# Attention scores: the order of the four matmuls in a group

## The chip, the cores and the metric

The kernel runs on one core of a Trainium2 chip. The metric is the device time of one execution, in microseconds (us); of several executions the median is given.

## The reference, cut to what matters

A gated cross-attention layer with a mixture of experts behind it, on 8 batches of 512 tokens with 256 features, in float32:

```
q, k, v = heads of layernorm(x) @ Wq + bq, ctx @ Wk + bk, ctx @ Wv + bv   # 16 heads of 16 features
attn = softmax(clip(q @ k.T / 4, -10000, 10000))
x = x + tanh(g_xattn) * ((attn @ v) @ Wo + bo)
x = x + tanh(g_ffn) * experts(layernorm(x))      # 8 experts, gated with a threshold over all tokens
```

The change lies in the scores, `q @ k.T`. The experts, which take most of the time, are the same in both kernels.

## The kernel before, in words

The program has stages with a barrier between them: a projection (`build_project`), attention (`build_attend`), two stages that only run when a flag asks for them, and the experts (`build_experts`). In the profile attention lies between about 105 and 577 us.

Attention goes through 8 batches (`b`), in each through 4 groups of 4 heads (`g`), and in each group through 4 steps (`k`, one for each block of 128 keys). Each step needs two kinds of score for the 4 heads of a group:

- A transposed score, T0 to T3 (`scores_T`, line 825): 128 keys by 512 queries into a bank of `ps_t`. ScalarE takes its exponential into `probs_T` (line 1072), and this frees the bank. There are three banks, so a T waits for the exponential of the third T before it (semaphore `exp_done`).
- A plain score, S0 to S3 (`scores`, line 815), for the group that comes two groups later: 128 queries by 512 keys into a bank of `ps_s`. VectorE reduces it to its row minimum (line 958), which later serves to keep the exponentials in range, and this frees the bank. Here too are three banks, so an S waits for the reduction of the third S before it (`low_done`).

Both have a contraction of 48 or 49 rows and take only half of the array's rows: even heads lie on rows 0 to 63 and odd heads on rows 64 to 127 (`half_rows`). Two matmuls on different halves can run at the same time. The plain scores take the heads in the order 1, 0, 3, 2 (`SCORE_HEADS`), so S0 lies on the upper half, and S1 on the lower one.

TensorE's order is written out by hand (lines 906 to 930). A step is: a first four of matmuls (T0, S0, T1, S1), the product of the previous step's probabilities with the values (`probs_v`, line 836, eight matmuls), a shared unit if there is one, a second four (T2, S2, T3, S3), and again a shared unit if there is one. TensorE works through this list in its order; a matmul that waits holds those behind it.

A shared unit is a small piece of work that isn't scores and that uses one common bank, `ps_m`: transposing the minima (`low`, line 842), the output heads (`out`, 847), the attention rows (`rows`, 853), the output projection (`y`, 861), transposes of the residual stream (`x2T`, 868, and `xnT`, 874), and the gate's logits (882, 889). The table `SHARED` says after which half step each one stands. Each waits until the unit before it has been taken out of the bank by ScalarE or VectorE. VectorE's own queue is in order too: in each step two reductions, then what it takes of a shared unit (`normalise`, line 981; `add_residual`, 991; `layer_norm`, 1008; `split`, 1016), then two more reductions. ScalarE has two exponentials, its unit, and two exponentials.

Of the kernel before, what the change touches and what calls it, by code (L numbers as in the profile page):

```python
# [55 lines left out]
def wait(eng, sem, value):  # L56

    if isinstance(value, int) and value <= 0:
        return
    eng.wait_ge(sem, value)  # L60
# [505 lines left out]
def exists(b):  # L566

    return not isinstance(b, int) or 0 <= b < BATCH
# [20 lines left out]
def half_rows(j, rows):  # L589

    return slice(j % 2 * 64, j % 2 * 64 + rows)


def group_after(b, g, steps):

    return b + (g + steps) // GROUPS, (g + steps) % GROUPS


def bank_of(turn, at):

    return (turn + at) % BANKS


def turn_after(turn, g, steps):

    return turn + (g + steps) // GROUPS
# [9 lines left out]
def build_attend(nc, io, scratch, keep):  # L616
    with ExitStack() as ctx:
# [61 lines left out]
        def group_no(b, g):  # L679
            return b * GROUPS + g  # L680

        def free_after(b, at):

            return b * PRODUCTS + at - BANKS + 1
# [121 lines left out]
        def _(pe):  # L806
            def scores(b, g, t, i, turn):

                at = (g * TT + t) * GROUP + i
                j = SCORE_HEADS[i]  # L810
                rows = half_rows(j, ROWS)
                if t == 0 and i == 0:
                    pe.wait_ge(qk_loaded[g], b * QK_PIECES * 16 + QK_PIECES * 16)
                wait(pe, low_done, free_after(b, at))
                pe.matmul(ps_s[bank_of(turn, at)][:], q_st[g][rows, j // 2, t * P:(t + 1) * P], k_st[g][rows, j // 2, :],  # L815
                          start=True, stop=True).then_inc(scores_in_psum, 1)

            def scores_T(b, g, k, j, turn):

                at = (g * TT + k) * GROUP + j  # L820
                if k == 0 and j == 0:
                    pe.wait_ge(rows_sent, group_no(b, g) * 32 + 32)
                wait(pe, exp_done, free_after(b, at))
                rows = half_rows(j, ROWS + 1)
                pe.matmul(ps_t[bank_of(turn, at)][:], k_st[g][rows, j // 2, k * P:(k + 1) * P], q_st[g][rows, j // 2, :],  # L825
                          start=True, stop=True).then_inc(t_in_psum, 1)

            def probs_v(b, g, k):

                n = quad_no(b, g, k)  # L830
                if k == 0:
                    pe.wait_ge(v_loaded[g], b * 16 + 16)
                    wait(pe, o_copied, group_no(b, g))
                pe.wait_ge(exp_done, n * GROUP + GROUP)
                for j in range(GROUP):
                    mm = pe.matmul(ps_o[32 * j:32 * j + VW, :], v_st[g][:, k, j, :], probs_T[k][:, j, :],  # L836
                                   start=(k == 0), stop=(k == TT - 1))
                mm.then_inc(pv_done, 1)
# [57 lines left out]
            def shared(b, unit):  # L896
                if not unit or not exists(b + unit[1]):
                    return
                kind, off, i = unit
                before = unit_before(b, unit)  # L900
                if before:
                    pe.wait_ge(taken[before[0]], before[1] + 1)
                write[kind](bank(kind, b + off, i), b + off, i).then_inc(in_psum[kind], 1)

            def batch(b, turn):
                for g in range(GROUPS):
                    ahead, turn_ahead = group_after(b, g, 2), turn_after(turn, g, 2)
                    for k in range(TT):
                        back = (b, g, k - 1) if k else (*group_after(b, g, -1), TT - 1)
                        more = exists(ahead[0]) and exists(b)  # L910
                        if exists(b):
                            scores_T(b, g, k, 0, turn)
                        if more:
                            scores(*ahead, k, 0, turn_ahead)
                        if exists(b):
                            scores_T(b, g, k, 1, turn)
                        if more:
                            scores(*ahead, k, 1, turn_ahead)
                        if exists(back[0]):
                            probs_v(*back)  # L920
                        shared(b, SHARED.get((g, k, 0)))
                        if exists(b):
                            scores_T(b, g, k, 2, turn)
                        if more:
                            scores(*ahead, k, 2, turn_ahead)
                        if exists(b):
                            scores_T(b, g, k, 3, turn)
                        if more:
                            scores(*ahead, k, 3, turn_ahead)
                        shared(b, SHARED.get((g, k, 1)))  # L930

# [6 lines left out]
            pe.wait_ge(o_zeroed, 1)  # L938
            pe.wait_ge(consts_set, 11)
            batches(pe, batch)  # L940
            pe.wait_ge(fits_summed, 1)
            pe.matmul(ps_m[:, 0:1], ones[:], fits_sum[:], start=True, stop=True).then_inc(fits_in_psum, 1)
# [1747 lines left out]
```

## Time and profile before

| | us |
|---|---|
| median of 3 runs | 2020.22 (2015.19 to 2020.96) |
| profiled execution, its own time | 2026.49 |
| its span in the profile | 2024.7 |
| one batch in steady attention | 56.0, with a stretch at half clock 58.6 |
| PE, DVE and ACT busy in the whole span | 94%, 66%, 61% |

PE is TensorE's matmuls, PEld its weight loads, DVE is VectorE and ACT is ScalarE. The number in brackets behind a row of the timeline is the time in which the engine stood idle before it, and behind the arrow what released it. Since weights are loaded ahead, the idle time of PEld is no loss by itself; its start, though, shows when a matmul was allowed to go.

### The profile page before, as it was taken

What the parts mean: (1) busy time and instruction counts of PE and PEld (TensorE: products, weight loads), DVE (VectorE), ACT (ScalarE), POOL (GpSimd) and SP (SyncE); (2) the same over time, 40 slices, a digit from 0 to 9 for tenths busy, and PEclk for the clock granted to TensorE, in tenths of its full rate; (3) what the DMA queues carried; (4) which work ended last, traced back from release to release, by engine and by line L of the source; (5) the groups of instructions that cost most, each with busy time, mean ns of one, the idle gap of its engine ahead of it and who ended that gap; (6) DMA issues with size and microseconds to landing.
All of it is one profiled execution on the core that took longest, in us unless ns stands there. A gap on an engine that the chain in (4) does not pass through costs nothing.

```text
span 2024.7 us, 26015 instructions
## 1 busy us (share of the span) xinstructions
PE 1909.2 (94%) x8916; PEld 1361.0 (67%) x8916; DVE 1341.9 (66%) x2333; ACT 1239.8 (61%) x2076; POOL 162.2 (8%) x334
## 2 busy tenths in 40 slices
PE   6999999999967989999999999999999999999998
PEld 5743333333435767788878878878887887887886
DVE  5588888888618886555755666565575566656555
ACT  3437777776722222576666667676676666767664
POOL 4300011110105530000000000000000000000000
PEclk9969999999968999999999999999999999999999
DMA  6833323222101325224222242322423224332221
GB/s 235 328 117 85 86 72 80 76 76 69 46 22 44 145 96 187 104 89 167 98 105 105 88 163 100 109 104 84 167 100 109 105 83 155 111 110 83 105 104 52
DMA packets 97259, 220.81 MB, mean 109 GB/s; under 512 B 31330, under 2 KB 49508, under 8 KB 87908
## 3 DMA queue, kind: packets, MB, share of 16 engines
q1 hardware_dynamic: 97124, 219.12, 31.6%
q8 instruction: 71, 1.16, 0.2%
q14 instruction: 64, 0.52, 0.1%
HBM read 178.57 MB, written 40.24 MB: 108 GB/s over the span
## 4 chain that ended last, share of the span: by engine, by line
PE 60%; DVE 4%; ACT 2%; POOL 2%; issue 1%; SPq 0%; DMA 0%; DVEq 0%; ACTq 0%
PE ps_y L2111 29%; PE ps_h L2058 25%; PE ps_y L2030 3%; PE ps_h L2016 3%; DVE h_lo L2384 1%; ACT gelu L2273 1%; DVE w_pair L2510 1%; ACT w_pair L2244 1%; DVE h_hi L2380 1%; DVE early L2518 1%; DVE out_T_acc L2461 1%; SPq L1829 0%; ACT h_hi L2276 0%; DVE gated L2454 0%; DMA gates_scratch<-gate 0%
## 5 line engine op out<-in xcount | busy, mean ns | idle before, releaser
L2384 DVE TENSOR_TENSOR h_lo<-gelu,h_hi 128x512 fp32r<-128x512 f32 x512 | 360.5, 709 | 415.1 <-ACT h_hi L2276 414.0
L2058 PE MATMUL ps_h<-x_hi,w_pair 128*128 128x512 f32 x1568 | 568.4, 396 | 11.2 <-ACT gelu L2273 9.4
L2273 ACT ACTIVATE gelu<-early,b 128x512 f32<-128x512 f32 x336 | 243.9, 726 | 237.4 <-DVE early L2518 229.3
L2111 PE MATMUL ps_y<-h_hi,w_hi 128*128 128x512 f32 x896 | 354.8, 396 | 3.5 <-DVE h_lo L2384 3.5
L2058 PEld LDWEIGHTS ps_h<-x_hi,w_pair 128*128 128x128 f32 x1568 | 294.8, 188 | 89.2 <-issue 13.0
L2111 PE MATMUL ps_y<-h_hi,w_lo 128*128 128x512 f32 x896 | 354.6, 396 | 0.0
L2111 PE MATMUL ps_y<-h_lo,w_hi 128*128 128x512 f32 x896 | 353.9, 395 | 0.0
L958 DVE TENSOR_REDUCE low<-ps_s 128x1 f32<-128x512 f32 x512 | 322.4, 685 | 35.1 <-PE ps_s L815 31.9
L2276 ACT ACTIVATE h_hi<-gelu 128x512 fp32r<-128x512 f32 x448 | 284.1, 634 | 43.3 <-ACT gelu L2273 2.6
L2058 PE MATMUL ps_h<-x_lo,w_pair 128*128 128x512 f32 x784 | 309.2, 394 | 0.0
L1072 ACT ACTIVATE probs_T<-ps_t 128x512 f32<-128x512 f32 x384 | 208.0, 601 | 107.9 <-PE ps_t L825 106.4
L2518 DVE TENSOR_TENSOR early<-ps_h,copy 128x512 f32<-128x512 f32 x336 | 230.7, 687 | 52.8 <-PE ps_h L2058 52.7
L815 PE MATMUL ps_s<-k_st,q_st 48*128 48x512 f32 x512 | 206.9, 484 | 3.0 <-SPq L733 2.0
L825 PE MATMUL ps_t<-q_st,k_st 49*128 49x512 f32 x512 | 194.3, 464 | 7.0 <-ACT probs_T L1072 4.7
L2111 PEld LDWEIGHTS ps_y<-h_hi,w_hi 128*128 128x128 f32 x896 | 168.4, 188 | 44.4 <-DVE h_lo L2384 3.9
L2111 PEld LDWEIGHTS ps_y<-h_hi,w_lo 128*128 128x128 f32 x896 | 168.5, 188 | 40.6
L2111 PEld LDWEIGHTS ps_y<-h_lo,w_hi 128*128 128x128 f32 x896 | 169.0, 189 | 39.1
L825 PEld LDWEIGHTS ps_t<-q_st,k_st 49*128 49x128 f32 x512 | 81.1, 192 | 133.3 <-ACT probs_T L1072 75.7
L2058 PEld LDWEIGHTS ps_h<-x_lo,w_pair 128*128 128x128 f32 x784 | 147.2, 188 | 34.7
L2208 ACT ACTIVATE gelu<-ps_h,b 128x512 f32<-128x512 f32 x64 | 44.1, 689 | 126.4 <-PE ps_h L2016 104.0
L836 PE MATMUL ps_o<-probs_T,v_st 128*17 128x512 f32 x768 | 103.5, 611 | 1.2 <-ACT probs_T L1072 1.2
L815 PEld LDWEIGHTS ps_s<-k_st,q_st 48*128 48x128 f32 x512 | 85.2, 196 | 19.1 <-DVE low L958 15.7
(247 smaller groups left out, 2150.8 us busy)
## 6 DMA issues: line engine op xcount, KB each, us to landing
x_hi<-blocks_scratch SPq DMA_DIRECT2D x28, 1024.0 KB, 5.1
x_lo<-blocks_scratch SPq DMA_DIRECT2D x28, 1024.0 KB, 8.8
x_hi<-blocks_scratch SPq DMA_DIRECT2D x28, 768.0 KB, 6.7
x_lo<-blocks_scratch SPq DMA_DIRECT2D x28, 768.0 KB, 10.2
gate<-gates_scratch SPq DMA_DIRECT2D x64, 256.0 KB, 3.2
q_st<-q_scratch SPq DMA_DIRECT2D x192, 64.0 KB, 2.4
k_st<-k_scratch SPq DMA_DIRECT2D x192, 64.0 KB, 2.4
k_scratch<-k_hl SPq DMA_DIRECT2D x8, 1024.0 KB, 3.9
```

The lines of the kernel that those rows point to most:

```text
L815: pe.matmul(ps_s[bank_of(turn, at)][:], q_st[g][rows, j // 2, t * P:(t + 1) * P], k_st[g][rows, j // 2, :], start=True, stop=True).then_in ...
L825: pe.matmul(ps_t[bank_of(turn, at)][:], k_st[g][rows, j // 2, k * P:(k + 1) * P], q_st[g][rows, j // 2, :], start=True, stop=True).then_in ...
L836: mm = pe.matmul(ps_o[32 * j:32 * j + VW, :], v_st[g][:, k, j, :], probs_T[k][:, j, :], start=(k == 0), stop=(k == TT - 1))
L958: dve.tensor_reduce(low[:, g % 2, column:column + 1], ps_s[bank_of(turn, at)][:], AX_X, ALU.min).then_inc(low_done, 1)
L1072: act.activation(probs_T[k][:, j, :], ps_t[bank_of(turn, (g * TT + k) * GROUP + j)][:], ACT.Exp, scale=-1.0).then_inc(exp_done, 1)
L2016: mm = pe.matmul(ps_h[:, j % RING, :], w[:, k, at], x[:, k, bass.ds(c * SEQ, SEQ)], start=(i == 0), stop=(i == len(parts) - 1))
L2058: mm = pe.matmul(bank, w[wp], x[xp], start=start and n == 0, stop=n == 2, skip_group_check=not start)
L2111: mm = pe.matmul(ps_y[s][:, d, :], w[:, j, at], h[:, c, :], start=(i == 0 and c < 2 and m == 0), stop=(i == QUADS - 1 and c >= 2 and m == 2))
L2273: act.activation(gelu[:, c % GELUS, :], src, ACT.Gelu_apprx_tanh, bias=b1[p][:, j:j + 1]).then_inc(gelu_done, 1)
L2276: act.activation(h_hi[:, c, :], gelu[:, c % GELUS, :], ACT.Copy).then_inc(h_hi_done, 1)
L2384: dve.tensor_tensor(h_lo[:, j % RING, :], gelu[:, j % GELUS, :], h_hi[:, j % RING, :].bitcast(F32), ALU.subtract).then_inc(h_ready, 1)
L2518: dve.tensor_tensor(corner[c // 2], bank, copies[0 if c == 3 else 1][:], ALU.add).then_inc(corner_done, 1)
```

## The change

In a four of matmuls, the two transposed scores now come first and the two plain ones after them: (T0, T1, S0, S1) in place of (T0, S0, T1, S1), and so in the second four. The waits, banks, halves of the array and the other engines' queues stay as they are.

```diff
                         if exists(b):
                             scores_T(b, g, k, 0, turn)
+                            scores_T(b, g, k, 1, turn)
                         if more:
                             scores(*ahead, k, 0, turn_ahead)
-                        if exists(b):
-                            scores_T(b, g, k, 1, turn)
-                        if more:
                             scores(*ahead, k, 1, turn_ahead)
                         if exists(back[0]):
                             probs_v(*back)
                         shared(b, SHARED.get((g, k, 0)))
                         if exists(b):
                             scores_T(b, g, k, 2, turn)
+                            scores_T(b, g, k, 3, turn)
                         if more:
                             scores(*ahead, k, 2, turn_ahead)
-                        if exists(b):
-                            scores_T(b, g, k, 3, turn)
-                        if more:
                             scores(*ahead, k, 3, turn_ahead)
                         shared(b, SHARED.get((g, k, 1)))
```

## Rows read from the trace of the kernel before

**Rows 1.** The stretches view, one row a batch: engines' busy time, clock, DMA
```profile
core 0: us, PE busy (x) PEld busy (x) DVE busy (x) ACT busy (x) POOL busy (x), PEclk, DMA share, GB/s
229.90:285.90 56.00, 52.29 (x330) 21.92 (x328) 48.68 (x97) 39.93 (x80) 6.06 (x16) 1.00 0.30 77
285.90:344.50 58.60, 55.04 (x332) 22.68 (x328) 48.85 (x98) 40.28 (x80) 6.04 (x16) 0.94 0.28 74
```

**Rows 2.** The waits, from 126 to 572 us: total us, times, longest
```profile
DVE low L958 <- PE ps_s L815: 31.0, 60, 1.7
PE ps_t L825 <- ACT probs_T L1072: 4.7, 21, 0.5
PEld ps_m L868 <- DVE attn L981: 4.1, 7, 0.6
PEld ps_m L842 <- DVE x_res L991: 5.0, 7, 0.7
PE ps_m L874 <- DVE xn_b L1008: 5.3, 6, 0.9
```

**Rows 3.** The timeline, two fours with nothing late: start, us, engine, line
```profile
238.64 0.49 PE L825 MATMUL ps_t<-q_st,k_st 49*128 49x512 f32 x1
238.65 0.29 PEld L815 LDWEIGHTS ps_s<-k_st,q_st 48*128 48x128 f32 x2
238.98 0.40 PE L825 MATMUL ps_t<-q_st,k_st 49*128 49x512 f32 x1
239.17 1.09 ACT L1072 ACTIVATE probs_T<-ps_t 128x512 f32<-128x512 f32 x2
239.21 1.95 DVE L958 TENSOR_REDUCE low<-ps_s 128x1 f32<-128x512 f32 x3 [0.35 <-PE ps_s L815]
239.90 0.29 PEld L815 LDWEIGHTS ps_s<-k_st,q_st 48*128 48x128 f32 x2
240.23 0.40 PE L815 MATMUL ps_s<-k_st,q_st 48*128 48x512 f32 x1
```

**Rows 4.** Timeline of weight loads, the four with late T1 and S1
```profile
230.49 0.18 PEld L825 LDWEIGHTS ps_t<-q_st,k_st 49*128 49x128 f32 x1 [0.65 <-ACT probs_T L1072]
230.62 0.18 PEld L815 LDWEIGHTS ps_s<-k_st,q_st 48*128 48x128 f32 x1
231.05 0.13 PEld L836 LDWEIGHTS ps_o<-probs_T,v_st 128*17 128x17 f32 x8 [0.25 <-ACT probs_T L1072]
```

**Rows 5.** The same, at the next two places where T1 waits
```profile
233.31 0.18 PEld L825 LDWEIGHTS ps_t<-q_st,k_st 49*128 49x128 f32 x1 [0.21 <-ACT w_raw L1072]
233.35 0.18 PEld L815 LDWEIGHTS ps_s<-k_st,q_st 48*128 48x128 f32 x1
233.86 0.16 PEld L836 LDWEIGHTS ps_o<-w_raw,v_st 128*17 128x17 f32 x8 [0.33 <-issue]
...
262.06 0.18 PEld L825 LDWEIGHTS ps_t<-q_st,k_st 49*128 49x128 f32 x1 [0.49 <-ACT w_raw L1072]
262.61 0.16 PEld L836 LDWEIGHTS ps_o<-w_raw,v_st 128*17 128x17 f32 x8 [0.37 <-issue]
```

**Rows 6.** The timeline, DVE and weight loads: reductions that a shared unit stands behind
```profile
244.81 1.29 DVE L958 TENSOR_REDUCE low<-ps_s 128x1 f32<-128x512 f32 x2 [1.41 <-PE ps_s L815]
246.01 0.74 DVE L991 SCALAR_TENSOR_TENSOR x_res<-ps_m,tanh_g,x_res 128x512 f32<-128x512 f32 x1
246.81 0.09 PEld L842 LDWEIGHTS ps_m<-ident,low 128*16 128x16 f32 x1 [0.72 <-DVE x_res L991]
...
254.46 0.42 DVE L981 TENSOR_TENSOR attn<-ps_m,recip 128x256 f32<-128x256 f32 x1
254.94 0.42 PEld L868 LDWEIGHTS ps_m<-ident,x_res 128*128 128x128 f32 x4 [0.58 <-DVE attn L981]
```

**Rows 7.** The timeline of DVE, from 252.9 and from 263.9 us
```profile
252.28 1.99 DVE L958 TENSOR_REDUCE low<-ps_s 128x1 f32<-128x512 f32 x3
...
264.20 2.54 DVE L958 TENSOR_REDUCE low<-ps_s 128x1 f32<-128x512 f32 x4
267.28 0.73 DVE L1008 TENSOR_SCALAR xn_b<-x_res,moments_b 128x256 f32<-128x256 f32 x2
```

**Rows 8.** The timeline after the last plain score: two transposed scores alone
```profile
551.61 0.50 PE L825 MATMUL ps_t<-q_st,k_st 49*128 49x512 f32 x2
```

**Rows 9.** The timeline of weight loads, a four whose S1 waits for DVE
```profile
256.19 0.18 PEld L815 LDWEIGHTS ps_s<-k_st,q_st 48*128 48x128 f32 x1 [0.36 <-DVE low L958]
256.61 0.13 PEld L836 LDWEIGHTS ps_o<-probs_T,v_st 128*17 128x17 f32 x8 [0.24 <-issue]
```

## The prediction

> **What bounds it now.** I read first the busy times over slices of the span. TensorE is busy 94% of it, and everything after attention hangs behind a barrier, so what attention loses or gains goes into the time in full. Then one row for each batch of attention [rows 1]: 56.0 us, of which PE is busy 52.3, DVE 48.7 and ACT 39.9. No engine is full. PE works in a fixed order and stops briefly where DVE or ACT is behind; DVE has the smaller margin of these two. Last I read the timeline of one batch, PE's weight loads above all, since the start of a load shows when its matmul was allowed to go. Six batches repeat within 0.1 us at full clock, so one batch is enough, times seven: in the first there are no units of a batch before it, and in the last the plain scores end halfway.
>
> **What the change removes, adds and moves.** No instruction is added or removed, and no DMA moves. Within a four, T1 goes ahead of S0. I take it in parts.
>
> *The four itself, with nothing late.* Before, T0 and S0 start together and last 0.49 us; the second pair (T1, S1) starts 0.34 later and lasts 0.40 [rows 3]. After, the halves of the array are the same at each place in the list (lower, upper, upper, lower), and only the tensors trade places. Two transposed scores alone, after the last plain score, already run side by side in the trace: two of them in 0.50 us together [rows 8]. So a four takes PE as long as before: 0. The first pair's results come 0.49 after the start, the second pair's 0.34 + 0.40 = 0.74 after it. So T1 is ready 0.24 to 0.25 earlier and S0 0.24 later. That is the whole change.
>
> *What T1's 0.24 is worth.* T1 arrives at 238.98 + 0.40 = 239.38. ACT starts its two exponentials at 239.17, and two take 1.09 while one takes 0.60, so the second starts at 239.66 [rows 3]: 0.28 after its data. ACT, not T1, sets it. Gain: 0. Its bounds: 0, and the gain that the first rival below works out.
>
> *What S0's 0.24 costs.* DVE starts on S0 at 239.21, 0.07 after its data (238.65 + 0.49), and had been idle for 0.35 [rows 3]. After, it starts 0.24 later. Alone this costs nothing, as long as DVE catches up; it costs where PE next waits for a bank which that reduction frees, or for a unit that stands behind it in DVE's queue. I went through the 32 fours of a batch with two questions: did DVE start on S0 at once, and how long before its use is S1's bank free in the next four? These places remain.
>
> (a) T1 and S1 both late, in the last step of a batch and the first of the next. S1's load at 230.62 goes when the reduction of the former four's S0 ends, and `probs_v` follows at 231.05 [rows 4]. That reduction started on fresh data, so S1 goes at 230.86, and all behind it 0.24 later. S0, which now queues behind the late T1, starts at 230.49 + 0.22 = 230.71, and so isn't what decides; S1 does. 14 times 0.24 = 3.4 us.
>
> (b) In step 1 of group 0, S1's load at 233.35 likewise waits for such a reduction, and becomes 233.59. A product behind a late S1 starts 0.42 after that load [rows 9], so 234.01 in place of 233.86 [rows 5]: 0.15, seven times, 1.1 us. At 262.06, where T1 is late and S1's bank has been free for 0.3, S0 and S1 now follow T1 by 0.22, and the product can start 0.22 + 0.34 later, at 262.62. It started at 262.61 anyway [rows 5]: 0.
>
> (c) Where the shared unit between two fours is short, S1's bank becomes free 0.10 ahead of its load: the reduction from 239.21 ends at 239.90, and the second load of plain scores is at 240.00 [rows 3]. After, 240.14, with the load at 240.18. That is before its matmul's turn at 240.23, but a matmul lasts 0.50 from a fresh load and 0.40 from one made ahead, so it ends 0.06 later. Three places in a batch, 22 in all: 1.4 us. In the other fours the bank has been free for 0.24 or more, or DVE was behind at the former S0 and wouldn't see the delay, as at 256.19 [rows 9].
>
> (d) Units behind the reductions. The pair of reductions at 244.81 starts 0.17 after its data, so 0.14 later after the change; the residual (L991) follows it without a gap, and the transposes of L842 wait for that with 0.35 of real idleness (0.72 less the 0.37 that a finished four leaves) [rows 6]. 0.14. The reductions from 252.28 on run without a gap into L981, for which L868 waits [rows 6, 7]: the one at 252.98 starts as its data comes, so 0.24. The four reductions from 264.20 run without a gap to L1008 at 267.28, and L874 waits for that [rows 2, 7]: 0.24. Each occurs seven times, as the counts of these waits say, 7, 7 and 6 [rows 2]. 7 x 0.62 = 4.3 us. The units that wait for ScalarE's part (L1016 behind L1100) have 0.3 us in hand on DVE: 0.
>
> Sum: 3.4 + 1.1 + 1.4 + 4.3 = 10.2 us slower. Nothing in the four gives any of it back. The price of S0's delay is bounded below by 0, if PE's own order always hides it. It is bounded above by every case in which DVE stood idle and waited for a plain score: 60 times [rows 2], 60 x 0.24 = 14.4 us. If all 240 fours with plain scores paid, it would be 58; but the 32 fours of the batch looked at show that most don't, and I take the count by places.
>
> *The clock.* Two of the seven batches hold a stretch at half clock (1.2 instead of 2.4 GHz, mean 0.94) and last 58.6 us, 2.6 longer [rows 1]; PE had pauses in the same places in the others, which kept full clock. The change makes three of these pauses longer, at the end and start of a batch. A rule of the Trainium skill bears on this (TensorE: Matmul & The Clock Gate, section HAM oscillation): pauses of TensorE between bursts bring it back to half clock, and each return costs. The trace agrees that half-clock stretches come where PE stops and starts; no row says how near the other batches are. My sum leaves the clock as it is; by the rule it would be the third rival's.
>
> The sum belongs to the profiled execution: 2026.5 + 10.2 = 2036.7. This execution was 6.3 us (0.3%) above the median of the runs, so for the median I say 2020.2 + 10.2 = 2030.
>
> **The rivals.**
>
> *Faster: the exponentials do come earlier.* If ScalarE's second exponential is set by T1 after all, each comes up to 0.24 earlier. It decides where PE waits for ACT: T1's bank at 230.49, 233.31 and 262.06 and in the last step, four places a batch [rows 4, 5], and 21 such waits in the table [rows 2]. If DVE then hides S0's delay, the gain is 28 x 0.24 = 6.7 us: 2013. Against it: 0.28 us of waiting of finished data in rows 3.
>
> *No change: the delay is hidden.* If (d) doesn't come through, because PE is held by something else at those units, and (a) is absorbed by ScalarE, whose exponential releases `probs_v` at 231.05 too [rows 4], 2 to 5 us remain: 2020 to 2025. For it: half of the sum hangs on DVE running without gaps from a reduction to a unit.
>
> *Slower by more: half clock in most batches.* If the five other batches fall to half clock as well, 5 x 2.6 = 13 us on top: 2043. For it: the two batches that do show nothing else that is different.
>
> **How the numbers follow.** I give the forecast (7 to 16 us slower) 0.50, hidden 0.25, faster 0.09, more half clock 0.16. About 0.3%, 6 us, is what a measurement of this kernel can tell from no change. The hidden case ends within that, and so does a quarter of the faster one's; a part of the forecast's lower end might be measured as no change as well. Faster by over 0.3%: 0.07; within: 0.27; slower: 0.66. The range runs from the faster rival, 2013, to the third one with the 3 us by which runs differ, 2046. The likeliest case's own range is 2024 to 2038.
>
> **What would show it.** In the changed kernel's timeline a four should be two L825 together, then two L815 0.34 later, with the loads in the same places (else the first step is wrong). ACT's pairs should still last 1.09. DVE's wait for plain scores, 31.0 us in 60 [rows 2], should rise by 10 to 20 us. A batch should take 57.4 instead of 56.0, with the additions at 231.05, 233.86, 246.81, 254.94 and 268.12. A batch of 56.0 or less refutes the forecast; more batches at 58.6 or longer with clock 0.94 speak for the third rival. If batches last 57.4 and the time doesn't rise, the loss is given back behind the barrier, for which I see no mechanism.

## The result, and the profile after

| | before | changed |
|---|---|---|
| median of the timed runs | 2018.89 us (4 runs) | 2034.79 us (4 runs) |
| ratio | | 1.0067, 95% interval 1.0046 to 1.0087 |
| ratio, measured once more (17 and 6 runs) | | 1.0088, 1.0065 to 1.0112 |
| profiled execution, its span and mean clock | 2024.7 us, 0.972 | 2028.2 us, 0.978 |
| a batch of attention at full clock | 56.0 | 57.4 |

The ratios put the change at 13 to 18 us slower (they aren't the quotients of the medians shown: for the first row that is 1.0079, 15.9 us); 2030 was forecast. The two profiled executions differ by only 3.5 us, and that is not the change's effect: in the changed kernel's profile the clock was higher. What the change does is seen where both run at full clock. The stretches view, two rows of six, one row a batch, with the columns of [rows 1]:

```profile
173.40:230.80 57.40, 53.25 (x330) 23.07 (x328) 48.88 (x97) 39.92 (x80) 7.61 (x17) 1.00 0.28 75
...
402.90:463.00 60.10, 55.96 (x331) 23.72 (x328) 48.91 (x97) 40.16 (x80) 6.06 (x16) 0.94 0.28 72
```

A batch went from 56.0 [rows 1] to 57.4 us with DVE's and ACT's busy times unchanged: they wait more. PE's own busy time rose from 52.3 to 53.3 with the same matmuls, because late ones that lay side by side now follow each other; so most of the loss isn't to be found as idle time of PE. Whether the order costs PE something in every four is a rival, tested below. One of the six batches, at mean clock 0.94, took 60.1; before it was two of six.

The four of matmuls is what the prediction described. The timeline of the changed kernel at the place of [rows 3] (the reduction is now L954 and the exponential L1068, four lines up):

```profile
297.23 0.19 PEld L825 LDWEIGHTS ps_t<-q_st,k_st 49*128 49x128 f32 x2 [0.85 <-ACT probs_T L1068]
297.23 0.50 PE L825 MATMUL ps_t<-q_st,k_st 49*128 49x512 f32 x2
297.33 0.19 PEld L815 LDWEIGHTS ps_s<-k_st,q_st 48*128 48x128 f32 x2
297.56 0.40 PE L815 MATMUL ps_s<-k_st,q_st 48*128 48x512 f32 x2
297.76 1.09 ACT L1068 ACTIVATE probs_T<-ps_t 128x512 f32<-128x512 f32 x2
298.00 1.94 DVE L954 TENSOR_REDUCE low<-ps_s 128x1 f32<-128x512 f32 x3 [0.36 <-PE ps_s L815]
```

T0 and T1 start together, S0 and S1 0.33 later. The exponentials start 0.53 after the four and last 1.09, as before: ScalarE makes nothing of the earlier T1. DVE starts 0.77 after the four, against 239.21 - 238.64 = 0.57 [rows 3]: 0.20 later. In the table of waits, from 126 to 575 us:

```profile
DVE low L954 <- PE ps_s L815: 44.2, 99, 1.5
PEld ps_m L868 <- DVE attn L977: 5.5, 7, 0.8
PEld ps_m L842 <- DVE x_res L987: 6.5, 7, 0.9
PE ps_m L874 <- DVE xn_b L1004: 6.0, 6, 1.0
```

DVE waits for plain scores 99 times and 44.2 us, where it was 60 times and 31.0 [rows 2]. But only some of this reaches TensorE. The sums for L868 and L842 rose by 1.4 and 1.5 us over seven waits, 0.2 each.

The weight loads of the four with late T1 and S1 (case (a)), then those behind the units of case (d), and the late S1 at the place (2,2):

```profile
288.77 0.18 PEld L825 LDWEIGHTS ps_t<-q_st,k_st 49*128 49x128 f32 x1 [0.65 <-ACT probs_T L1068]
288.88 0.41 PEld L815 LDWEIGHTS ps_s<-k_st,q_st 48*128 48x128 f32 x2
289.54 0.13 PEld L836 LDWEIGHTS ps_o<-probs_T,v_st 128*17 128x17 f32 x8 [0.25 <-issue]
...
305.61 0.09 PEld L842 LDWEIGHTS ps_m<-ident,low 128*16 128x16 f32 x1 [0.92 <-DVE x_res L987]
313.95 0.20 PEld L868 LDWEIGHTS ps_m<-ident,x_res 128*128 128x128 f32 x2 [0.79 <-DVE attn L977]
...
324.42 0.18 PEld L815 LDWEIGHTS ps_s<-k_st,q_st 48*128 48x128 f32 x1 [0.16 <-DVE low L954]
```

In (a) the product (L836) comes 0.77 after T1's load, where it was 231.05 - 230.49 = 0.56 [rows 4]. The waits in (d) are 0.92 and 0.79, where they were 0.72 and 0.58 [rows 6].

To see where, I took the interval from one four to the next, at each of the 32 places of a batch, as the median over the six batches from the second to the seventh (fours at half clock left out), and subtracted that of before, in us:

```
place (group, step, half)    what stands behind it          predicted  measured
(0,0) first                  S1 late, (a)                   0.24       0.21
(0,1) first                  S1 late, (b)                   0.15       0.09
(0,3), (2,0) first           S1's bank just free, (c)       0.06 each  0.02 each
(1,0) second                 L842 waits for DVE, (d)        0.14       0.21
(1,2) second                 L868 waits for DVE, (d)        0.24       0.21
(2,1) first                  T1 late                        0          0.06
(2,2) first                  S1's bank just free, (c)       0.06       0.21
(2,2) second                 L874 waits for DVE, (d)        0.24       0.13
(3,3) first                  S1 late, (a)                   0.24       0.20
the other 22                                                0          -0.01 to 0.01 each
a batch                                                     1.43       1.33
```

### The profile page after: what moved, and what is told of

It reads as the page before. It is cut to its first block, busy times and chain, and to the rows that moved or that the text cites. A ratio compares the mean times of both kernels' runs of the same rounds, so it can differ in the third digit from the quotient of the medians.

```text
span 2028.2 us, 26015 instructions
## 1 busy us (share of the span) xinstructions
PE 1906.6 (94%) x8916; PEld 1365.9 (67%) x8916; DVE 1343.1 (66%) x2333; ACT 1236.5 (61%) x2076; POOL 161.9 (8%) x334
## 4 chain that ended last, share of the span: by engine, by line
PE 60%; DVE 4%; ACT 2%; POOL 2%; issue 1%; SPq 0%; DMA 0%; DVEq 0%; ACTq 0%
PE ps_y L2107 29%; PE ps_h L2054 25%; PE ps_y L2026 3%; PE ps_h L2012 3%; ACT gelu L2269 1%; DVE h_lo L2380 1%; DVE w_pair L2506 1%; ACT w_pair L2240 1%; DVE early L2514 1%; DVE out_T_acc L2457 1%; DVE h_hi L2376 0%; SPq L1825 0%; ACT h_hi L2272 0%; DMA gates_scratch<-gate 0%; DVE gated L2450 0%
## 5 line engine op out<-in xcount | busy, mean ns | idle before, releaser
L954 DVE TENSOR_REDUCE low<-ps_s 128x1 f32<-128x512 f32 x512 | 324.1, 685 | 46.4 <-PE ps_s L815 45.1
L1068 ACT ACTIVATE probs_T<-ps_t 128x512 f32<-128x512 f32 x384 | 207.8, 601 | 111.3 <-PE ps_t L825 110.2
L2514 DVE TENSOR_TENSOR early<-ps_h,copy 128x512 f32<-128x512 f32 x336 | 230.6, 686 | 53.6 <-PE ps_h L2054 53.3
L2107 PEld LDWEIGHTS ps_y<-h_hi,w_hi 128*128 128x128 f32 x896 | 168.3, 188 | 44.2 <-DVE h_lo L2380 3.9
L825 PE MATMUL ps_t<-q_st,k_st 49*128 49x512 f32 x512 | 147.1, 499 | 7.4 <-ACT probs_T L1068 5.2
L825 PEld LDWEIGHTS ps_t<-q_st,k_st 49*128 49x128 f32 x512 | 56.6, 186 | 131.8 <-ACT probs_T L1068 77.5
L815 PE MATMUL ps_s<-k_st,q_st 48*128 48x512 f32 x512 | 129.3, 435 | 3.2 <-SPq L733 2.0
L836 PE MATMUL ps_o<-probs_T,v_st 128*17 128x512 f32 x768 | 102.7, 607 | 1.2 <-ACT probs_T L1068 1.2
L2282 ACT ACTIVATE copy<-ps_h 128x512 f32<-128x512 f32 x112 | 66.7, 596 | 51.1 <-PE ps_h L2054 50.9
## 6 DMA issues: line engine op xcount, KB each, us to landing
x_lo<-blocks_scratch SPq DMA_DIRECT2D x28, 768.0 KB, 10.1
```

The costliest lines, as they stand in the source:

```text
L954: dve.tensor_reduce(low[:, g % 2, column:column + 1], ps_s[bank_of(turn, at)][:], AX_X, ALU.min).then_inc(low_done, 1)
L1068: act.activation(probs_T[k][:, j, :], ps_t[bank_of(turn, (g * TT + k) * GROUP + j)][:], ACT.Exp, scale=-1.0).then_inc(exp_done, 1)
L2107: mm = pe.matmul(ps_y[s][:, d, :], w[:, j, at], h[:, c, :], start=(i == 0 and c < 2 and m == 0), stop=(i == QUADS - 1 and c >= 2 and m == 2))
L2282: act.activation(copies[0][:], x, ACT.Copy).then_inc(copied, 1)
L2514: dve.tensor_tensor(corner[c // 2], bank, copies[0 if c == 3 else 1][:], ALU.add).then_inc(corner_done, 1)
```

## The experiments

Each kernel differs from the one before in the order of a four alone, unless it is said otherwise. Where it varies by place, the code is this, with the set of places `PAIRED`:

```diff
+                        def four(i, j, paired):
+                            order = [("T", i), ("T", j), ("S", i), ("S", j)] if paired else [("T", i), ("S", i), ("T", j), ("S", j)]
+                            for kind, n in order:
+                                if kind == "T" and exists(b):
+                                    scores_T(b, g, k, n, turn)
+                                if kind == "S" and more:
+                                    scores(*ahead, k, n, turn_ahead)
```

**The change once more.** No edit.

> The changed kernel once more. Place by place, its profile showed 57.36 us for a batch of attention against 56.03 before, which is 9.3 us over seven batches; its timed runs showed 13 to 16. Theory A (the rest is the clock: which stretches fall to half clock varies from run to run): the ratio comes nearer to 1.005, its interval holds 1.0046 (9.3 us), and the batches at full clock take 57.3 to 57.4 again. Theory B (the change also makes more half-clock stretches): the ratio stays at 1.0067 or above, and the profile shows more of them than the two in the seven batches of the kernel before.

Measured: ratio 1.0088 (1.0065 to 1.0112); batches at full clock 57.36 to 57.41 us; one of six with a stretch at half clock (58.7). So 9.3 us over seven batches isn't the whole loss, and it isn't chance that it looked larger; but the profile shows no more half-clock stretches in attention than that of before. Theory A fell, and B isn't shown by one profile. More on this below, where the first and the last batch are counted too.

**Where the loss comes from: eleven fours against the other 21.**

```diff
+PAIRED = {(0, 0, 1), (0, 2, 1), (1, 0, 0), (1, 2, 0), (1, 3, 1), (2, 0, 1), (2, 1, 0), (2, 1, 1), (2, 2, 0), (3, 2, 1), (3, 3, 1)}
+                        four(0, 1, (g, k, 0) in PAIRED)
...
+                        four(2, 3, (g, k, 1) in PAIRED)
```

(Each is group, step, half; in the complement, `not in`.)

> The new order only in eleven of a batch's 32 fours: those whose delayed first plain score, by my account, something waits for (the bank of a late S1 in the next four, or a shared unit behind the reductions); the old order in the other 21. Theory A (the loss comes through these waits): nearly all of it, a batch of 57.1 to 57.4 us, 8 to 10 us slower in all. Rival (each four in the new order costs the same, by its order on TensorE itself: 1.33/32 = 0.042 us): 11 x 0.042 = 0.46, a batch of 56.5 us, 3 us slower in all.

> The complement: the new order in the other 21 fours, the old one in the eleven. Theory A: nothing waits for these, so a batch of 56.0 to 56.15 us and a time within 0.1% of the kernel before. Rival (the same price for each four): 21 x 0.042 = 0.88, a batch of 56.9 us, 6 us slower in all.

Measured: ratio 1.0063 (1.0043 to 1.0083) for the eleven, some 13 us where 8 to 10 were expected, and 1.0013 (0.9998 to 1.0028) for the 21. One batch of the eleven, then one of the 21:

```profile
232.00:289.36 57.36, 53.25 (x330) 22.71 (x328) 48.48 (x97) 39.91 (x80) 6.05 (x16) 1.00 0.28 75
```

```profile
404.70:461.00 56.30, 52.59 (x330) 22.05 (x328) 48.88 (x97) 39.92 (x80) 6.05 (x16) 1.00 0.29 77
```

In a steady batch the eleven bring the whole 1.33 us, at the same places and by the same amounts (within 0.02) as the full change. The fixed price for each four is refuted: eleven would have cost 0.46. The 21 were to cost 0.15 at most and cost 0.28. All of it stands at the three fours with a late T1 and S1: there, even when S1's bank is in time, S0 queues behind T1 on the same half of the array. Its matmul starts 0.34 after T1's (at 174.31, after 173.97), and the product follows 0.33 behind it. The loads of such a four in the 21:

```profile
173.97 0.18 PEld L826 LDWEIGHTS ps_t<-q_st,k_st 49*128 49x128 f32 x1 [0.65 <-ACT probs_T L1067]
174.08 0.21 PEld L816 LDWEIGHTS ps_s<-k_st,q_st 48*128 48x128 f32 x2
174.63 0.13 PEld L837 LDWEIGHTS ps_o<-probs_T,v_st 128*17 128x17 f32 x8 [0.35 <-ACT probs_T L1067]
```

The product (L837 here) comes 0.66 after T1's load, against 231.05 - 230.49 = 0.56 [rows 4]. So 0.10 of the price is the queue behind T1. In the full change S1's load, late by its bank, and S0's matmul come at the same time, and the product follows the fresh load later still: the two don't add, the larger one counts, 0.20.

**First fours or second fours alone.** `four(0, 1, False)` and `four(2, 3, True)`, then the reverse.

> The new order only in the second four of each step. Theory A: the places in which a first four's S1 waits for the bank freed by the second four's S0 (0.21, 0.09 and 0.20 us at the three places with a late T1, and a few hundredths where the unit between is short) remain, the units behind VectorE's reductions don't: a batch of 56.5 to 56.7 us. Rival (it is the units behind the reductions that cost): 56.1 or less.

> The new order only in the first four of each step. Theory A: the delays of the shared units behind the reductions remain (L842 0.2, L868 0.2, L874 0.15 to 0.24) and the late banks of S1 go: a batch of 56.6 to 56.75 us, and L842, L868 and L874 late by these amounts. Rival (it is S1's banks that cost): 56.1 or less.

Measured, in one run each: 56.7 us for the second fours, as expected (0.21, 0.09 and 0.21 at the three places), but with 0.12 at L874, where nothing was expected. For the first fours 57.1 us, more than expected: L842 and L868 0.21 each, as expected, but also 0.10, 0.07, 0.08 and 0.10 at the four places where T1 is late, which the account had put at nothing, and 0.21 at (2,2), where I had looked for it in the second fours. The rivals, for which 56.1 or less would have spoken, fall in both. 0.63 and 1.10 add to more than 1.33, since both kinds meet in the same waits: L874 is 0.12 late in either kernel, and 0.13 in the full change.

**With short reductions.** Old and new order, with half of each plain score reduced:

```diff
-                dve.tensor_reduce(low[:, g % 2, column:column + 1], ps_s[bank_of(turn, at)][:], AX_X, ALU.min).then_inc(low_done, 1)
+                dve.tensor_reduce(low[:, g % 2, column:column + 1], ps_s[bank_of(turn, at)][:, 0:SEQ // 2], AX_X, ALU.min).then_inc(low_done, 1)
```

> The old order, with VectorE's reductions over the first 256 of the 512 keys only (a reduction is then shorter; the other half of the minimum is left out). This is the base for the next run: a batch shorter than 56.0, 54 to 55.7 us, since the waits of S1 and of L991, L981 and L1008 shrink.

> The new order, with the same reductions over half of the keys. Theory A (the loss comes from VectorE starting later on S0, where something waits for it): with VectorE well ahead, S1's bank is free long before it is needed, so a batch is at most 0.3 to 0.9 us longer than in the old order with such reductions, and what remains stands at the four places with a late T1, where the plain scores queue behind it. Rival (the order costs on TensorE itself, in all fours): 1.3 us longer, as with full reductions.

One run each. A batch in the old order, then in the new one:

```profile
221.40:275.70 54.30, 51.32 (x332) 21.37 (x328) 32.67 (x98) 39.85 (x80) 6.06 (x16) 1.00 0.32 79
```

```profile
222.50:277.60 55.10, 52.12 (x331) 21.96 (x328) 32.50 (x97) 39.81 (x80) 6.06 (x16) 1.00 0.31 78
```

The windows are rounded; by the starts of the fours they are 54.24 and 55.08, so 0.84 longer, at the upper end of what was expected. DVE was busy 32.6 us instead of 48.7. Of the loss, what hung on S1's banks at (0,3), (2,0) and (2,2) is gone, and so is that at L842 and L868 (0.03 and 0.01 are left). There remain 0.17, 0.07, 0.07 and 0.17 at the places with a late T1, and 0.21 at L874, which still stands in DVE's queue; 0.06 and 0.04 are new, in the first fours of (1,1) and (1,3). Theory A holds in kind: a faster DVE takes away the part that came through DVE. It isn't a proof for each place, since the last one stayed.

**Plain scores first.** `order` is S0, S1, T0, T1 in all fours.

> The mirror image: the two plain scores first, then the two transposed ones (S0, S1, T0, T1). Theory A: now T0 is 0.24 us late, and ScalarE, which starts on it within 0.1 us of its data in most fours, starts 0.24 later; the banks of T1 that come late (four places) and the products behind the exponentials come later, and VectorE gains nothing, since S1 already waited for it: a batch of 57.0 to 58.5 us, so slower than the kernel before as well. Rival (VectorE is what bounds attention, and to serve it first pays): a batch under 56.0 us.

```profile
183.50:243.20 59.70, 53.84 (x329) 22.38 (x331) 48.68 (x98) 40.32 (x80) 7.66 (x17) 1.00 0.28 73
```

```profile
PEld ps_s L815 <- DVE low L952: 112.2, 171, 1.7
```

59.7 us, above my range, and 2061.8 in one run against 2024.03. ScalarE's later start is there: behind the four at 190.51 the exponentials start at 191.34, 0.83 later, against 240.49 - 239.89 = 0.60 at that place before. But the larger part is another one. S1 now stands ahead of both transposed scores, and when its bank is late, T0 and T1 wait as well. The loads of such a four:

```profile
239.13 0.18 PEld L815 LDWEIGHTS ps_s<-k_st,q_st 48*128 48x128 f32 x1 [0.75 <-DVE low L952]
239.24 0.22 PEld L825 LDWEIGHTS ps_t<-q_st,k_st 49*128 49x128 f32 x2
```

The 112.2 us in the table overstate it: a plain score is now the first load of a four, and its row takes in the pause of 0.85 us that follows every product and that stood at the transposed scores before. Counted load by load, S1's load came over 0.06 us behind the loads ahead of it in 60 of 240 fours, 38 us together; in the kernel before in 46 of 240, 14 us together. The rival, that serving DVE first pays, is refuted clearly. The Trainium skill (TensorE: Matmul & The Clock Gate, Part 3: Packing small matmuls, The mechanism) says that matmuls on different parts of the array still start and end in program order. This run agrees as to the starts: one of T0 and T1 lies on the half that S1 doesn't use, and both follow S1; the ends in the trace are modelled. The same section lists that a weight load overlaps with running matmuls only on different rows, while its text also allows it for a background buffer. Against the list's "only", the loads at 297.33 above lie inside the matmuls of 297.23 to 297.73, on the same two halves. The measurement decides.

**The rest of the loss.** Each timed run has a mean clock c and a span s. The clock has two levels in the traces, full and half, so 2(1 - c)s is the run's time at half clock. Over 90 timed runs, of the seven kernels that ran more than once with their clock on record (the runs of before in the table on top have none), a common line fits with 1.1 us of scatter: each us at half clock costs 0.34 us. The last column is the time that this line gives for 100 us at half clock, called the time at equal clock; the figures behind +- are standard errors:

```
kernel                    runs  mean us  at half clock (us)  us at equal clock
before (both series)      36    2022.5   102.5 +- 1.4        2021.7
the change                10    2036.6   112.8 +- 4.6        2032.3
the eleven                6     2034.1   109.1 +- 3.9        2031.0
the other 21              12    2024.7   100.2 +- 3.2        2024.6
last fours (below)        12    2026.6   105.0 +- 2.6        2025.0
not at the seam (below)   8     2031.3   104.0 +- 4.0        2030.0
logits later (below)      6     2033.4   117.8 +- 4.2        2027.3
```

The change costs 10.6 us at equal clock. That is more than the 9.3 of seven batches at 1.33, and the traces show where the rest is: there are eight batches, and the first one loses more than a steady one. In it the units of a batch before are missing, so that more fours stand back to back, and the fours behind them lose about 0.2 each: at (1,0), (1,3), (2,0), (2,3) and (3,0), as (3,3) does in every batch. Its 25 fours that ran at full clock in both profiles lose 1.5 us, the last batch 0.8, and the six between 8.0: 10.4 together. For the other 21 the same count gives 2.9, as at equal clock (2024.6 - 2021.7); for the eleven 9.9 against 9.3.

The other 3.5 us of the change's 14.1 are 10 us more at half clock. In the profiles, the half-clock stretches of the steady batches began within 2 us of the start of a batch, near the two pairs of fours that stand back to back. What TensorE did ahead of one doesn't tell it apart: in the kernel before it was busy 1.49 of the 1.7 us from 285.9, after which the clock fell to half, and 1.49 of the 1.7 us from 229.9, after which it stayed full. So I asked whether the longer stops there bring them.

```diff
+PAIRED = {(3, 2), (3, 3)}
+                        four(0, 1, False)
...
+                        four(2, 3, (g, k) in PAIRED)
```

(and the reverse, both halves, `not in {(3, 2), (3, 3), (0, 0)}`.)

> The new order only in two fours of a batch, the second ones of its last two steps; after them come the two fours with a late T1 and S1, at the end of a batch and the start of the next, and each should be held 0.20 us longer. What is open is the second part of the loss: over the timed runs so far, the changed kernel spent 113 us at half clock (from the mean clock of each run), the kernel before 99. All half-clock stretches within attention began 1 to 2 us after the start of a batch. Theory A (the longer stops of TensorE at the seam of two batches bring them): a batch at full clock takes 56.4 us, the time at equal clock rises by 3 us, and the half-clock time is nearer to 113 than to 99. Rival (the half-clock time grows with the length of attention or by chance): 99 to 102 us at half clock.

> The reverse: the new order everywhere but in the last two steps of a batch and the first of the next. Theory A: the seam is as in the kernel before, so 99 to 103 us at half clock; a batch at full clock of 56.9 to 57.0 us, and at equal clock 6 to 7 us slower. Rival (length or chance): 106 to 113 us at half clock, since two thirds of the loss are still there.

Measured: ratios 1.0016 (1.0005 to 1.0028) and 1.0042 (1.0026 to 1.0057). Batches at full clock:

```profile
229.10:285.60 56.50, 52.74 (x332) 22.04 (x328) 48.68 (x97) 39.98 (x80) 6.06 (x16) 1.00 0.31 76
```

```profile
233.10:290.10 57.00, 52.84 (x332) 22.57 (x328) 48.88 (x98) 39.96 (x80) 6.06 (x16) 1.00 0.29 76
```

By the fours' starts 56.43 and 56.95: the account by places holds again, 0.40 and 0.92. At equal clock they are 3.3 and 8.3 us slower, where 3 and 6 to 7 were expected (2.7 and 7.4 by the count of all eight batches). The half-clock time, 105.0 and 104.0, doesn't tell them apart, and the kernel before had 105.3 beside these two and 99.3 beside the runs above. The theory of the seam is not shown, nor is its rival. That the change brings more half clock at all rests on 112.8 +- 4.6 against 102.5 +- 1.4. It stays open.

**An attempt to fill the stops.**

```diff
-    (3, 1, 0): ("out", 0, 2), (3, 1, 1): ("logits", -1, 0), (3, 3, 0): ("pick", -1, 0),
+    (3, 1, 0): ("out", 0, 2), (3, 2, 1): ("logits", -1, 0), (3, 3, 0): ("pick", -1, 0),
```

> The order of the kernel before, but the gate's logits (a shared unit) one step later, behind the second four of step 2 in group 3. There two fours stand back to back, and T1 and S1 of the latter are late by 0.5 and 0.6 us; the unit, 1.1 us long, would fill that wait. Expected if this wait is lost time: 0.6 us less in a batch, unless the next unit (pick), which needs ScalarE's copy of the logits, now holds TensorE in its place. With the copy behind two exponentials, pick would wait until 1.65 + 0.6 us after the start of the last step's first four, against 1.65 when its turn comes, so 0.65 late: then no gain, or a loss of 0.1. I take no difference, 2019 to 2024 us, as the likelier. Fewer stops at the seam could lessen the half-clock time.

```profile
397.71 0.18 PEld L825 LDWEIGHTS ps_t<-q_st,k_st 49*128 49x128 f32 x1 [0.65 <-ACT probs_T L1072]
398.00 0.18 PEld L815 LDWEIGHTS ps_s<-k_st,q_st 48*128 48x128 f32 x1
...
403.47 0.97 PEld L889 LDWEIGHTS ps_m<-pick,logits_T 128*128 128x128 f32 x8 [1.48 <-ACT logits_T L1105]
```

Ratio 1.0051 (1.0031 to 1.0071), a batch of 56.57 at full clock: 0.54 slower, and more time at half clock. No difference was expected, or 0.1 in a batch. `pick` waits 1.48 - 0.85 = 0.63 us longer, as worked out. What I had overlooked is in the first line: where the unit was taken away, two fours now stand back to back in their turn, and the late T1 only moved there. Eight batches at 0.54 are at most 4.3 us, and the time at equal clock rose by 5.6; where the rest is stays open. No kernel with the full reductions beats the one before.

## Why the prediction was right, point by point

- *What bounds attention.* Right: no engine is full, and the loss is time in which PE waits for DVE by way of a bank or of a shared unit. In a steady batch the eleven fours carry all of it.
- *The four itself.* Right: same length for PE, T1 earlier, S0 later, by 0.20 at DVE for the 0.24 that the matmuls' ends gave.
- *T1's 0.24 is worth nothing.* Right: exponentials still start 0.53 after the four and last 1.09. The faster rival falls.
- *(a)* Right in cause and size, 0.21 and 0.20 for 0.24. One term inside was too small: S0 was to start 0.22 behind the late T1, and its matmul starts 0.34 behind (its load 0.11). That alone costs 0.10 at the product, as the 21 fours show; in the change the late S1 covers it.
- *(b)* 0.09 for 0.15, the same mechanism. At (2,1), named with 0, it was 0.06: the same 0.22 was too small here.
- *(c)* Two of the three places were nearly free, 0.02. The third, (2,2), was 0.21: DVE came to it already late from the fours before, so that its reductions ran 0.4 later against the four than before the change (0.28 ahead of it instead of 0.68). The account had taken each four by itself. Its 22 places at 0.06 are also 1.3 us, not 1.4, and the sum 10.1.
- *(d)* L842 0.21 for 0.14, L868 0.21 for 0.24, L874 0.13 for 0.24. At L842 the reduction started 0.17 after its data, and 0.10 of this was taken for slack. It wasn't: after the change there are still 0.13 between data and start (303.61, after 303.48). At (2,2), (c) and (d) together are 0.34 for 0.30.
- *The count of batches.* "Times seven" left the first one out for having no units of a batch before it. For just that reason it has more fours back to back, and loses 1.5 us. The last loses 0.8.
- *The upper bound.* 60 waits of DVE for a plain score were taken as every case that could pay. After the change there are 99: a reduction that followed the one before it without a pause can come to wait as well. The bound of 14.4 us wasn't one.
- *The sum.* 10.2 us forecast; 10.4 by the places of all eight batches, 10.6 at equal clock. That it comes so close is partly luck: the errors by place (0.28 too low at three places, 0.35 too high at the others, in a batch) and the missing batch nearly cancel.
- *The clock.* Left out of the sum, for want of a row that says how near a batch is to half clock. The change's ten runs have 10 us more of it than the runs of before, 3.5 us of time, with a standard error of half that. So the forecast of 7 to 16 us slower holds the first measurement (15.9 by the medians) at its edge, and the second (16.5 by the medians) not, though the mechanism accounts for 10.4 only. The third rival, half clock in nearly all batches, didn't come true in either profile of the change: one of six each.

## What to carry to other kernels

In a queue that is worked through in order, a swap of two items that cost the same is not neutral: what moves is when each consumer starts, and it counts for the consumer that is idle and whose result is awaited. Look at both consumers' time from data to start: here 0.28 us on ScalarE's side for T1 made the gain worthless, and 0.07 on VectorE's side for S0 made the delay real. Then go by places, the first and the last round of a loop included: 22 of 32 cost nothing in a steady batch, delays that meet in one wait count once, and a delay can add up in the consumer's queue over several items. And before two profiles of a small change are compared as wholes, compare stretches at equal clock.

## What the runs showed of the hardware that I had not expected

- Mean clock explains most of the spread between executions of one kernel: 0.34 us of time for each us at half clock, with 1.1 us of scatter left, while the times of one kernel spread over 12 us. With it a difference of 3 us can be told (2024.6 against 2021.7).
- Two matmuls on the two halves of the array, followed by two more on the same halves, are 0.33 to 0.34 us apart at full clock, whichever tensors they read, though their weights were loaded 0.10 to 0.11 after the first pair's start (238.75 and 238.64 before, 297.33 and 297.23 after the change).
